# Copying the two halves of each tile's attention values through SP's DMA queue in place of POOL

## The chip, the cores and the metric

The kernel runs on one core of one Trainium2 chip. The metric is the device time of one execution in microseconds, as the median of several runs. The core has five engines with an instruction queue each: TensorE (PE, matmuls; PEld is its weight load), VectorE (DVE), ScalarE (ACT), GpSimd (POOL) and SyncE (SP, which here only issues DMAs). They meet through semaphores.

## The reference

Two blocks follow each other on x of 2 x 1024 x 128 float32, each with a layer norm ahead of and behind it and a residual sum: a gated linear attention, and two layers of local attention with a gated feed-forward part. The change lies in the local attention, 8 heads of 64, in windows of 64 tokens:

```python
def local_attention(q, k, v):
    b, h, n, d = q.shape
    w = n // WINDOW
    bq = q.reshape(b, h, w, WINDOW, d) * QK_SCALE
    bk = k.reshape(b, h, w, WINDOW, d)
    bv = v.reshape(b, h, w, WINDOW, d)
    def look_around(t):
        p = jnp.pad(t, ((0, 0), (0, 0), (1, 0), (0, 0), (0, 0)))
        return jnp.concatenate([p[:, :, :w], p[:, :, 1:]], axis=3)
    bk, bv = (look_around(bk), look_around(bv))
    ...
    sim = jnp.einsum('bhwid,bhwjd->bhwij', bq, bk)
    sim = jnp.where(mask, -jnp.finfo(sim.dtype).max, sim)
    attn = jax.nn.softmax(sim, axis=-1)
    out = jnp.einsum('bhwij,bhwjd->bhwid', attn, bv)
    return out.reshape(b, h, n, d)

def _layer(x, wqkv, qs, ksc, wo, lg, lb, w1, b1, w2, b2):
    h = shift_token(x)
    qkv = h @ wqkv
    ...
    o = local_attention(q, k, v)
    x = x + o @ wo
    h = shift_token(x)
    ...
    h = a * jax.nn.gelu(g, approximate=False)
    x = x + h @ w2 + b2
    return x

x = x + _layernorm(_L0_attn_ref(_layernorm(x), ...))
x = x + _layernorm(_L0_ffn_ref(_layernorm(x), ...))
```

Each window of queries looks at its own window of keys and values and at the one before it.

## The kernel before

Tokens are taken in tiles of 128 partitions, two windows of 64 each. The two batches alternate, so the 16 tiles of a layer are n = 0 to 15, and tile n - 2 holds the tokens ahead of tile n. The count over both layers is N = 16 l + n. The second window of a tile (partitions 64 to 127, w = 1 in `weigh_values`) looks at both halves of its own tile, which lie as they are in `v_cur`, one buffer for even and one for odd tiles, 8 heads of 64 columns and a column of ones (VC = 65), 520 columns. The first window (w = 0) looks at the first half of its own tile and the second half of tile n - 2; these are brought together in `v_mix`, four slots of 520 columns. The lower 64 partitions of a slot are filled from `v_cur` of tile n, the "own" half, and the upper 64 from `v_cur` of tile n - 2, the "past" half.

Every engine runs a fixed order, written by hand. For one tile, in steps k, the attention part is: TensorE projects q and k (two tiles ahead) and v (one ahead, `project_v`); ACT copies v from PSUM into `v_cur` (`copy_v_cur`, L1416); DVE rotates q and k (L1909), POOL adds the two rotated parts (`rotate_add`, L475) and scales them by the inverse norms of ACT (`scale_qk`, L483, after ACT's L1379); TensorE transposes them (L900), computes scores, DVE subtracts the row maxima, ACT takes exponentials, TensorE transposes the probabilities (L942), and `weigh_values` (L628 with `v_mix` and `v_cur`) multiplies them with the values. DVE divides by the row sums, TensorE transposes and projects the result (L967, L628 with `wo_sb`), and DVE adds it to the stream into `middle` (`add_attention`, L1971, which counts `mid_ready`). SP then copies `middle`, half of its columns shifted by one token, into `hcat` with three DMAs (L334 of 128 partitions, L336 of 127 and L338 of one), and from there the feed-forward part begins.

The copies into `v_mix` are two POOL instructions per tile: `mix_values` (L492) for the own half and `keep_values` (L503) for the past half, counted by `vlow_ready` and `vup_ready`. TensorE waits for them in `weigh_values`, and ACT in `copy_v_cur` before it overwrites a `v_cur` buffer. In a step POOL does `scale_qk`, the two copies, `normalise_z` (L511) and `rotate_add`, in that order.

The last two tiles of a layer (14 and 15) are not in the loop: in `drain` every engine interleaves them with the first hidden blocks of the feed-forward part. There TensorE's order is: `project_v(15)`, `scores(15)`, `weigh_values(14)`, `project_o(13)`, `transpose_probs(15)`, `transpose_o(14)`, `weigh_values(15)`, then `hidden_block(l, 0, 1)`, `transpose_o(15)`, `project_o(14)` and so on.

Of the kernel before, what the change touches and what calls it, by code (L numbers as in the profile page):

```python
# [24 lines left out]
def build_program(nc, x, Wq, Wk, Wv, Wg, Wgk1, Wgk2, bgk2, Wo, rms_w,  # L25
# [26 lines left out]
    with ctx:  # L52
# [53 lines left out]
        def tile_of(buf, n):  # L106
# [72 lines left out]

        d = sems("d_ident d_const d_masks d_x0 d_x1 d_x2 d_low d_qk d_vg d_out_w d_gcols d_rms d_qkv d_cols d_scales d_tab d_ffn d_even d_odd d_out")  # L180
        s = sems(
# [9 lines left out]
            "table_ready cos_ready xtr_done ht_ready qk_done rot_ready sq_ready ss_ready ssc_ready ssl_ready inv_ready "  # L191
            "add_ready qr_ready qkt_done qkt_ready v_done vcur_ready vlow_ready vup_ready sc_done max_ready sub_ready "
            "p_ready pt0_done pt1_done pt0_ready pt1_ready pv_done rec_ready on_ready ot_done ot_ready wo_done mid_ready "
# [80 lines left out]
        def _(sp):  # L274
# [39 lines left out]
            with nc.allow_non_contiguous_dma(reason="per-partition columns of the small vectors"):  # L314
# [3 lines left out]
                for l in range(DEPTH):  # L318
                    for half in range(2):
# [6 lines left out]
                                       ).then_inc(d["d_cols"], 16)  # L326

            for l in range(DEPTH):
                for n in range(NT):
                    N = NT * l + n  # L330
                    at = (n % 4) * D
                    sp.wait_ge(s["mid_ready"], N + 1)
                    wait(sp, s["zn_ready"], N - 3)
                    sp.dma_start(hcat[:, at:at + D // 2], middle[:, (n + 2) * D:(n + 2) * D + D // 2]  # L334
                                 ).then_inc(d[("d_even", "d_odd")[n % 2]], 16)
                    sp.dma_start(hcat[1:P, at + D // 2:at + D], middle[0:P - 1, (n + 2) * D + D // 2:(n + 3) * D]  # L336
                                 ).then_inc(d[("d_even", "d_odd")[n % 2]], 16)
                    sp.dma_start(hcat[0:1, at + D // 2:at + D], middle[P - 1:P, n * D + D // 2:(n + 1) * D]  # L338
                                 ).then_inc(d[("d_even", "d_odd")[n % 2]], 16)

            ov = res[:, :].rearrange("p (n d) -> p n d", d=D)
# [13 lines left out]
        def _(pool):  # L355
# [108 lines left out]
            for l in range(DEPTH):  # L464
# [20 lines left out]

                def mix_values(n, par):

                    N = base + n
                    W_ = AH * VC
                    wait(pool, s["vcur_ready"], N + 1)  # L490
                    wait(pool, s["pv_done"], N - 3)
                    pool.tensor_scalar(v_mix[0:W, (n % 4) * W_:(n % 4 + 1) * W_], v_cur[0:W, par * W_:(par + 1) * W_],  # L492
                                       1.0, 0.0, ALU.mult, ALU.add).then_inc(s["vlow_ready"], 1)

                def keep_values(n, par):

                    N = base + n
                    W_ = AH * VC
                    wait(pool, s["vcur_ready"], N + 1)
                    wait(pool, s["pv_done"], N - 1)  # L500
                    wait(pool, s["vlow_ready"], N + 1)
                    at = (n + 2) % 4 * W_
                    pool.tensor_scalar(v_mix[W:P, at:at + W_], v_cur[W:P, par * W_:(par + 1) * W_], 1.0, 0.0, ALU.mult, ALU.add  # L503
                                       ).then_inc(s["vup_ready"], 1)
                    wait(pool, s["vup_ready"], N + 1)

                def normalise_z(n, par):
# [6 lines left out]
                def step(k, par):  # L514
                    staged(scale_qk, k, par, 1)
                    staged(mix_values, k, par, 0)
                    staged(keep_values, k, par, 0)
                    staged(normalise_z, k, par, -3)
                    staged(rotate_add, k, par, 2)
                def attention_beside_last_pairs():  # L520
# [30 lines left out]
                    scale_qk(1, 1)  # L551
                    mix_values(0, 0)
                    keep_values(0, 0)
                    normalise_f(4, 0)
# [4 lines left out]
                    add_y(7, 1)  # L559
                    mix_values(1, 1)  # L560
                    keep_values(1, 1)
                    rotate_add(3, 1)
                    scale_qk(3, 1)
                    normalise_f(7, 1)
                    mix_values(2, 0)
                    keep_values(2, 0)
                    rotate_add(4, 0)
# [18 lines left out]
                pool.wait_ge(s["half_ready"], 1)  # L586
                pool.wait_ge(s["vup_ready"], base + NT)
                for n in (NT - 3, NT - 2, NT - 1):
                    rstd_of_z(n)
                    normalise_z(n, n % 2)  # L590
                if l + 1 < DEPTH:
                    pool.wait_ge(s["rot_ready"], base + NT)
                    pool.wait_ge(s["vup_ready"], base + NT)
                    for i in range(4):
                        cos_part(l + 1, i)
                        sin_part(l + 1, i)

            pool.wait_ge(s["vup_ready"], DEPTH * NT)

# [26 lines left out]
        def _(pe):  # L626
# [222 lines left out]
            for l in range(DEPTH):  # L849
# [95 lines left out]
                def weigh_values(n, par):  # L945
                    N = base + n
                    wait(pe, s["qkt_ready"], capped(N + 2, base + NT))
                    wait(pe, s["vcur_ready"], N + 1)
                    wait(pe, s["vlow_ready"], N + 1)
                    wait(pe, s["vup_ready"], base + max(n - 1, 0))  # L950
                    for a in range(2):
# [215 lines left out]
        def _(act):  # L1167
# [183 lines left out]
            for l in range(DEPTH):  # L1351
# [57 lines left out]
                def copy_v_cur(n, par):  # L1409
                    N = base + n  # L1410
                    wait(act, s["v_done"], N + 1)
                    wait(act, s["pv_done"], N - 1)
                    wait(act, s["vlow_ready"], N - 1)
                    wait(act, s["vup_ready"], N - 1)
                    o = v_cur[:, par * AH * VC:(par + 1) * AH * VC].rearrange("p (h e) -> p h e", e=VC)
# [811 lines left out]
```

## Time and profile before

| | us |
|---|---|
| median of 3 runs | 440.18 |
| lowest and highest | 439.87, 440.25 |
| the profiled execution | 440.01 |
| its span on the core | 437.9 |
| TensorE busy in the span | 409.5 |
| DVE busy | 339.5 |
| ACT busy | 305.5 |
| POOL busy | 292.6 |

Times within the trace are counted from the start of the span. A row of a timeline gives the start, the time taken, the engine, the line and the tensors written and read; what stands in brackets at its end is the idle time of the engine just ahead and what released it. Matmuls overlap each other, and the end of one is modelled, so a busy TensorE is not TensorE at its peak. The chain is the work that ended last, followed back from the end of the kernel to whatever released each piece.

### The profile page before, as it was taken

To read this page: it belongs to the slowest core of one execution; us is meant where nothing else is said; L and a number is where in the kernel's file an instruction comes from. 1 tells how busy PE (TensorE), PEld (TensorE's weight loads), DVE (VectorE), ACT (ScalarE), POOL (GpSimd) and SP (SyncE) were. 2 spreads that over 40 slices of the span, in tenths; PEclk is the share of its full clock that TensorE was granted. 3 is DMA by queue.
4 is the path that set the end of the run, shared out by engine and by line. 5 is a ranking of instruction groups with operands and counts; after the bars stand their busy time and mean duration, and the time that the engine had idled before them with its cause. 6 is when DMAs were issued, how large, how long until landed. Compare 5 with 4: busy or idle time off the path is not lost.

```text
span 437.9 us, 13201 instructions
## 1 busy us (share of the span) xinstructions
PE 409.5 (94%) x4851; PEld 291.2 (66%) x4851; DVE 339.5 (78%) x720; ACT 305.5 (70%) x677; POOL 292.6 (67%) x287
## 2 busy tenths in 40 slices
PE   3898999879999999999999999999999999999993
PEld 2566666656776777777766666677777777776563
DVE  3678867879898888988845377898889889855676
ACT  2677768758878887887773347678878878865322
POOL 3578957899978778776723536677777767761425
PEclk9999999999999999999999999999999999999998
DMA  7930000000000000000000000000000000000012
GB/s 190 327 70 3 2 3 3 3 1 2 8 15 8 7 13 9 8 12 10 7 7 14 0 2 2 7 8 8 12 10 7 11 12 8 8 8 13 8 35 61
DMA packets 21038, 10.37 MB, mean 24 GB/s; under 512 B 13236, under 2 KB 20208, under 8 KB 20976
## 3 DMA queue, kind: packets, MB, share of 16 engines
q1 hardware_dynamic: 20400, 9.14, 7.7%
q8 instruction: 40, 0.66, 0.6%
q10 hardware_dynamic: 576, 0.39, 0.3%
q14 instruction: 22, 0.18, 0.1%
HBM read 6.38 MB, written 1.05 MB: 17 GB/s over the span
## 4 chain that ended last, share of the span: by engine, by line
PE 73%; issue 5%; DVE 4%; ACT 3%; POOL 2%; DVEq 0%; POOLq 0%; ACTq 0%
PE psum L628 55%; PE psum L900 6%; PE psum L942 6%; PE psum L967 3%; PE psum L987 1%; PE psum L873 1%; ACT probs_t L1400 1%; DVE neg_max L1937 1%; POOL zn L511 1%; ACT qk_t L1387 1%; ACT sq L1368 0%; POOL rstd_z L578 0%; POOL ping L446 0%; PE psum L754 0%; DVE probs L1944 0%
## 5 line engine op out<-in xcount | busy, mean ns | idle before, releaser
L475 POOL TENSOR_TENSOR qr<-rot 128x1024 f32<-128x1024 f32 x32 | 75.8, 2367 | 29.4 <-DVE rot L1909 24.7
L628 PE MATMUL psum<-wqkv_sb,h_t 128*128 128x512 f32 x192 | 93.0, 595 | 0.0
L483 POOL TENSOR_TENSOR qr<-qr,inv 128x1024 f32<-128x1024 f32 x32 | 60.8, 1901 | 33.3 <-ACT inv L1379 33.2
L1917 DVE TENSOR_REDUCE ss<-sq 128x16 f32<-128x1024 f32 x32 | 39.0, 1219 | 14.8 <-ACT sq L1368 14.7
L1393 ACT ACTIVATE probs<-probs 128x512 f32<-128x512 f32 x64 | 39.4, 631 | 15.0 <-DVE probs L1944 14.6
L1937 DVE TENSOR_REDUCE neg_max<-psum 128x4 f32<-128x512 f32 x64 | 41.5, 685 | 10.4 <-PE psum L628 10.3
L628 PEld LDWEIGHTS psum<-v_mix,probs_t 128*64 128x64 f32 x512 | 32.2, 138 | 21.4 <-issue 19.8
L628 PE MATMUL psum<-z_t,w_sb 128*128 128x512 f32 (+1 forms) x96 | 44.7, 595 | 0.0
L628 PEld LDWEIGHTS psum<-wqkv_sb,h_t 128*128 128x128 f32 x192 | 31.7, 191 | 16.3 <-issue 16.2
L1944 DVE TENSOR_TENSOR probs<-psum,neg_max 128x512 f32<-128x512 f32 x64 | 41.3, 681 | 0.2
L1909 DVE TENSOR_TENSOR rot<-psum,cos_t 128x1024 f32<-128x1024 f32 x32 | 39.0, 1217 | 2.7 <-PE psum L628 2.4
L900 PEld LDWEIGHTS psum<-consts,qr 128*128 128x128 f32 x256 | 29.5, 141 | 16.5 <-POOL qr L483 10.9
L1337 ACT ACTIVATE gelu<-psum,columns 128x512 f32<-128x512 f32 (+1 forms) x24 | 16.4, 685 | 33.6 <-PE psum L628 33.5
L1909 DVE TENSOR_TENSOR rot<-psum,sin_t 128x1024 f32<-128x1024 f32 x32 | 38.8, 1214 | 0.0
L1368 ACT ACTIVATE sq<-psum 128x1024 f32<-128x1024 f32 x32 | 33.4, 1042 | 5.1 <-DVE rot L1909 5.1
L1880 DVE SCALAR_TENSOR_TENSOR hid<-psum,columns,gelu 128x512 f32<-128x512 f32 (+1 forms) x24 | 18.0, 749 | 24.2 <-ACT gelu L1337 24.2
L628 PE MATMUL psum<-v_cur,probs_t 128*64 128x65 f32 x512 | 36.7, 225 | 0.0
L628 PE MATMUL psum<-v_mix,probs_t 128*64 128x65 f32 x512 | 36.6, 225 | 0.1
L1407 ACT ACTIVATE o_t<-psum 128x512 f32<-128x512 f32 x32 | 19.1, 597 | 24.7 <-PE psum L967 23.3
L1387 ACT ACTIVATE qk_t<-psum 128x1024 f32<-128x1024 f32 x32 | 32.7, 1023 | 3.6 <-PE psum L900 2.0
L1400 ACT ACTIVATE probs_t<-psum 128x512 f32<-128x512 f32 x64 | 34.8, 598 | 0.5 <-PE psum L942 0.5
L942 PE MATMUL psum<-consts,probs 128*128 128x128 f32 x256 | 33.8, 274 | 1.4 <-ACT probs L1393 1.3
(150 smaller groups left out, 966.8 us busy)
## 6 DMA issues: line engine op xcount, KB each, us to landing
wqkv_sb<-in_L_ffn_wqkv SPq DMA_DIRECT2D x1, 1536.0 KB, 9.3
hcat<-middle SPq DMA_DIRECT2D x32, 32.0 KB
out_x<-pong SPq DMA_DIRECT2D x8, 128.0 KB, 1.8
hcat<-middle SPq DMA_DIRECT2D x32, 31.8 KB
x_in<-in_L_attn_x SPq DMA_DIRECT2D x2, 384.0 KB, 4.7
w_sb<-in_L_ffn_w SPq DMA_DIRECT2D x1, 682.0 KB
cos_base<-rotary_cos SPq DMA_DIRECT2D x1, 512.0 KB, 5.0
sin_base<-rotary_sin SPq DMA_DIRECT2D x1, 512.0 KB, 5.9
```

Of the source, the lines that this page charges most:

```text
L475: pool.tensor_tensor(o, a, b[:, :, ::-1, :], ALU.add).then_inc(s["add_ready"], 1)
L483: pool.tensor_tensor(a, a, inv[:, :].unsqueeze(2).to_broadcast([P, 2 * AH, DH]), ALU.mult).then_inc(s["qr_ready"], 1)
L628: return pe.matmul(o, w, m, start=start, stop=stop, skip_group_check=skip)
L900: ins = pe.transpose(p_turn[:, c * P:(c + 1) * P], qr[:, at:at + P], ident)
L942: ins = pe.transpose(p_sc[:, a * 512 + c * P:a * 512 + (c + 1) * P], probs[:, at:at + P], ident)
L1387: act.activation(qk_t[:, at:at + 2 * INNER], p_turn[:, :], ACT.Copy).then_inc(s["qkt_ready"], 1)
L1393: act.activation(p, p, ACT.Exp).then_inc(s["p_ready"], 1)
L1400: act.activation(probs_t[:, a * 512:(a + 1) * 512], p_sc[:, a * 512:(a + 1) * 512], ACT.Copy).then_inc(s[("pt0_ready", "pt1_ready")[a]], 1)
L1909: ins = dve.tensor_tensor(o[:, :].rearrange("p (i h e) -> p i h e", i=2, e=DH), x, tab.unsqueeze(2).to_broadcast([P, 2, AH, DH]), ALU.mult)
L1917: dve.tensor_reduce(ss[:, 0:4 * AH:2], sq[:, :].rearrange("p (h e) -> p h e", e=DH), AX.X, ALU.add).then_inc(s["ss_ready"], 1)
L1937: dve.tensor_reduce(neg_max[:, a * PAIRS:(a + 1) * PAIRS], heads_of(p_sc, a), AX.X, ALU.max, negate=True).then_inc(s["max_ready"], 1)
L1944: dve.tensor_tensor(heads_of(probs, a, par * AH * P), heads_of(p_sc, a), neg_max[:, a * PAIRS:(a + 1) * PAIRS].unsqueeze(2).to_broadcast([ ...
```

## The change

The two POOL instructions per tile are gone, with their semaphores and the waits on them. In their place SP issues two DMAs per tile (`spread_values`, with the same source and destination), each with a semaphore of its own for even and for odd tiles. Before each pair SP waits for `vcur_ready` of the tile and for `pv_done` of tile n - 2. Within a layer, SP's order is now the copies of tiles 0 and 1, then for each tile n its three `hcat` DMAs followed by the copies of tile n + 2. TensorE in `weigh_values` and ACT in `copy_v_cur` wait for the new semaphores in place of the old ones, at the same places.

```diff
+            def spread_values(l, n):
+                N = NT * l + n
+                W_ = AH * VC
+                own, past = n % 4 * W_, (n + 2) % 4 * W_
+                sp.wait_ge(s["vcur_ready"], N + 1)
+                wait(sp, s["pv_done"], N - 1)
+                sp.dma_start(v_mix[0:W, own:own + W_], v_cur[0:W, n % 2 * W_:(n % 2 + 1) * W_]
+                             ).then_inc(d[("d_own_even", "d_own_odd")[n % 2]], 16)
+                sp.dma_start(v_mix[W:P, past:past + W_], v_cur[W:P, n % 2 * W_:(n % 2 + 1) * W_]
+                             ).then_inc(d[("d_past_even", "d_past_odd")[n % 2]], 16)
+
             for l in range(DEPTH):
+                spread_values(l, 0)
+                spread_values(l, 1)
                 for n in range(NT):
...
                     sp.dma_start(hcat[0:1, at + D // 2:at + D], middle[P - 1:P, n * D + D // 2:(n + 1) * D]
                                  ).then_inc(d[("d_even", "d_odd")[n % 2]], 16)
+                    if n + 2 < NT:
+                        spread_values(l, n + 2)
...
-                def mix_values(n, par):
-                    N = base + n
-                    W_ = AH * VC
-                    wait(pool, s["vcur_ready"], N + 1)
-                    wait(pool, s["pv_done"], N - 3)
-                    pool.tensor_scalar(v_mix[0:W, (n % 4) * W_:(n % 4 + 1) * W_], v_cur[0:W, par * W_:(par + 1) * W_],
-                                       1.0, 0.0, ALU.mult, ALU.add).then_inc(s["vlow_ready"], 1)
-                def keep_values(n, par):
...
                 def step(k, par):
                     staged(scale_qk, k, par, 1)
-                    staged(mix_values, k, par, 0)
-                    staged(keep_values, k, par, 0)
                     staged(normalise_z, k, par, -3)
                     staged(rotate_add, k, par, 2)
...
                     wait(pe, s["vcur_ready"], N + 1)
-                    wait(pe, s["vlow_ready"], N + 1)
-                    wait(pe, s["vup_ready"], base + max(n - 1, 0))
+                    wait(pe, d[("d_own_even", "d_own_odd")[n % 2]], 16 * (N // 2 + 1))
+                    wait(pe, d[("d_past_even", "d_past_odd")[n % 2]], 16 * (N // 2))
...
                     wait(act, s["pv_done"], N - 1)
-                    wait(act, s["vlow_ready"], N - 1)
-                    wait(act, s["vup_ready"], N - 1)
+                    wait(act, d[("d_own_even", "d_own_odd")[n % 2]], 16 * (N // 2))
+                    wait(act, d[("d_past_even", "d_past_odd")[n % 2]], 16 * (N // 2))
```

SP's queue at the end of layer 0, before: the `hcat` DMAs of tiles 13 and 14, three each.

```order
79 L334 DMA hcat<-middle 128x64 [waits zn_ready,mid_ready]
80 L336 DMA hcat<-middle 127x64
81 L338 DMA hcat<-middle 1x16x4
82 L334 DMA hcat<-middle 128x64 [waits zn_ready,mid_ready]
83 L336 DMA hcat<-middle 127x64
84 L338 DMA hcat<-middle 1x16x4
```

The same place of SP's queue in the changed kernel: `hcat` of tile 13, the copies of tile 15, `hcat` of tile 14.

```order
106 L348 DMA hcat<-middle 128x64 [waits zn_ready,mid_ready]
107 L350 DMA hcat<-middle 127x64
108 L352 DMA hcat<-middle 1x16x4
109 L335 DMA v_mix<-v_cur 64x520 [waits pv_done,vcur_ready]
110 L337 DMA v_mix<-v_cur 64x520
111 L348 DMA hcat<-middle 128x64 [waits zn_ready,mid_ready]
112 L350 DMA hcat<-middle 127x64
113 L352 DMA hcat<-middle 1x16x4
```

The two copies of tile 15 now stand behind the wait for `mid_ready` of tile 13 and its three DMAs.

TensorE's queue in the same drain, before: the transposed probabilities of tile 15, the transposed output of tile 14, then the first matmuls of `weigh_values(15)`.

```order
719 L942 MATMUL psum<-consts,probs 128x128 [waits p_ready]
720 L942 MATMUL psum<-consts,probs 128x128 x3
721 L967 MATMUL psum<-consts,o_n 128x128 [waits ot_ready,vcur_ready,on_ready]
722 L967 MATMUL psum<-consts,o_n 128x128 x3
723 L628 MATMUL psum<-v_mix,probs_t 64x65 [waits vup_ready,vlow_ready,pt0_ready,vcur_ready,qkt_ready]
724 L628 MATMUL psum<-v_cur,probs_t 64x65
725 L628 MATMUL psum<-v_mix,probs_t 64x65
```

The same place of TensorE's queue in the changed kernel.

```order
719 L926 MATMUL psum<-consts,probs 128x128 [waits p_ready]
720 L926 MATMUL psum<-consts,probs 128x128 x3
721 L951 MATMUL psum<-consts,o_n 128x128 [waits ot_ready,vcur_ready,on_ready]
722 L951 MATMUL psum<-consts,o_n 128x128 x3
723 L612 MATMUL psum<-v_mix,probs_t 64x65 [waits d_past_odd,d_own_odd,pt0_ready,vcur_ready,qkt_ready]
724 L612 MATMUL psum<-v_cur,probs_t 64x65
725 L612 MATMUL psum<-v_mix,probs_t 64x65
```

Nothing moves on TensorE; the first `v_mix` matmul waits for `d_past_odd` and `d_own_odd` in place of `vup_ready` and `vlow_ready`.

POOL's queue in one step in the middle of layer 0, before (L373 makes a part of the rotary tables).

```order
110 L483 TENSOR_TENSOR qr<-qr,inv 128x1024 [waits inv_ready,add_ready]
111 L492 TENSOR_SCALAR v_mix<-v_cur 64x520 [waits vcur_ready]
112 L503 TENSOR_SCALAR v_mix<-v_cur 64x520 [waits vlow_ready,pv_done,vcur_ready]
113 L511 TENSOR_SCALAR zn<-hcat,mv_z,rstd_z 128x128 [waits z_rstd,vup_ready]
114 L475 TENSOR_TENSOR qr<-rot1,rot2 128x1024 [waits qkt_done,rot_ready]
115 L373 TENSOR_TENSOR cos_t<-cos_base,scales 128x256
116 L483 TENSOR_TENSOR qr<-qr,inv 128x1024 [waits inv_ready,add_ready]
```

The same step on POOL in the changed kernel.

```order
104 L499 TENSOR_TENSOR qr<-qr,inv 128x1024 [waits inv_ready,add_ready]
105 L506 TENSOR_SCALAR zn<-hcat,mv_z,rstd_z 128x128 [waits z_rstd]
106 L491 TENSOR_TENSOR qr<-rot1,rot2 128x1024 [waits qkt_done,rot_ready]
107 L389 TENSOR_TENSOR cos_t<-cos_base,scales 128x256
108 L499 TENSOR_TENSOR qr<-qr,inv 128x1024 [waits inv_ready,add_ready]
```

The two copies are gone from between the scaling and `zn`, and `zn` no longer waits for the second of them.

## Rows read from the trace of the kernel before

**Rows 1.** The page: busy times, and the shares of the chain by engine.

```profile
PE 409.5 (94%) x4851; PEld 291.2 (66%) x4851; DVE 339.5 (78%) x720; ACT 305.5 (70%) x677; POOL 292.6 (67%) x287
...
PE 73%; issue 5%; DVE 4%; ACT 3%; POOL 2%; DVEq 0%; POOLq 0%; ACTq 0%
```

**Rows 2.** The chain in order of time (start, us, what): q and k projections.

```profile
148.39 1.72 PE psum L628 x4
...
156.86 1.72 PE psum L628 x4
```

**Rows 3.** By tile, `v_mix` on POOL: count, ns min/median/max, first and last start.

```profile
L492 POOL TENSOR_SCALAR v_mix<-v_cur x32: 614/618/622, 98.6 to 391.5; 64x520 f32<-64x520 f32 x32
...
L503 POOL TENSOR_SCALAR v_mix<-v_cur x32: 622/624/629, 99.4 to 392.3; 64x520 f32<-64x520 f32 x32
```

**Rows 4.** Who waited for whom: us in total, times, longest us.

```profile
POOL qr L483 <- ACT inv L1379: 33.2, 29, 4.0
...
PE psum L900 <- POOL qr L483: 0.7, 1, 0.7
...
PEld psum L900 <- POOL qr L483: 10.9, 29, 0.6
```

**Rows 5.** Timeline of one middle tile of layer 0: start us, us, instruction.

```profile
136.65 0.63 ACT L1416 ACTIVATE v_cur<-psum 128x512 f32<-128x512 f32 x1
...
137.18 0.87 SPq L338 DMA_DIRECT2D hcat<-middle  x1
...
145.06 0.27 PE L628 MATMUL psum<-v_mix,probs_t 128*64 128x65 f32 x1
```

**Rows 6.** DMA issues: KB each, median us from issue to landing.

```profile
out_x<-pong SPq DMA_DIRECT2D x8, 128.0 KB, 1.8
...
wvg_sb<-in_L_attn_Wg ACTq DMA_DIRECT2D x1, 128.0 KB, 3.1
```

**Rows 7.** Timeline, start of layer 1: `v_cur` of tile 0, first use of `v_mix`.

```profile
268.14 0.60 ACT L1416 ACTIVATE v_cur<-psum 128x512 f32<-128x512 f32 x1 [0.49 <-PE psum L628]
...
272.53 0.24 PE L628 MATMUL psum<-v_mix,probs_t 128*64 128x65 f32 x1
```

**Rows 8.** Timeline, drain of layer 0: tiles 13 (DVE, SP) and 15 (PE).

```profile
225.57 0.28 DVE L1971 TENSOR_TENSOR middle<-psum,ping 128x128 f32<-128x128 f32 x1
...
227.11 0.87 SPq L338 DMA_DIRECT2D hcat<-middle  x1
...
226.56 0.27 PE L628 MATMUL psum<-v_mix,probs_t 128*64 128x65 f32 x1
```

**Rows 9.** Timeline, drain of layer 1: the same two.

```profile
397.44 0.88 SPq L338 DMA_DIRECT2D hcat<-middle  x1
...
396.89 0.27 PE L628 MATMUL psum<-v_mix,probs_t 128*64 128x65 f32 x1
```

**Rows 10.** DMA throughput in GB/s, 227 to 232 us in 40 equal slices.

```profile
GB/s 98 154 10 0 0 8 18 18 18 18 18 18 16 20 19 18 18 18 18 15 0 0 0 131 0 0 0 0 0 0 0 0 0 0 0 0 0 0 0 0
```

**Rows 11.** Stretches: length, busy PE, PEld, DVE, ACT, POOL, granted clock, DMA share, GB/s.

```profile
226.50:262.00 35.50, 35.50 (x193) 22.20 (x192) 18.30 (x36) 16.00 (x28) 13.11 (x16) 1.00 0.03 7
...
396.90:412.00 15.10, 15.10 (x100) 9.70 (x99) 8.56 (x25) 7.78 (x13) 3.62 (x6) 1.00 0.07 14
```

**Rows 12.** TensorE's last matmuls, and a later stretch (columns as in rows 11).

```profile
427.00 4.18 PE L628 MATMUL psum<-w_sb,hid 128*128 128x128 f32 x36
...
435.00:436.00 1.00, 0.00 (x0) 0.00 (x0) 0.23 (x1) 0.00 (x0) 0.09 (x1) 0.50 0.00 0
```

**Rows 13.** Timeline of TensorE in the first 24 us.

```profile
5.59 0.37 PE L638 MATMUL psum<-consts,wgk_sb 128*16 128x128 f32 x1 [5.59 <-DMA wgk_sb<-in_L_attn_Wgk]
...
8.78 1.22 PE L628 MATMUL psum<-middle,wgk_sb 128*128 128x256 f32 x2 [0.52 <-ACT middle L1199]
...
11.50 1.99 PE L628 MATMUL psum<-wvg_sb,middle 128*128 128x512 f32 x4
...
15.71 0.70 PE L628 MATMUL psum<-middle,wgk_sb 128*128 128x256 f32 x2
```

More of the change, by code:

```diff
@@ L177, in build_program @@
         xo, res = x_in, stream[DEPTH - 1]
-        d = sems("d_ident d_const d_masks d_x0 d_x1 d_x2 d_low d_qk d_vg d_out_w d_gcols d_rms d_qkv d_cols d_scales d_tab d_ffn d_even d_odd d_out")
+        d = sems("d_ident d_const d_masks d_x0 d_x1 d_x2 d_low d_qk d_vg d_out_w d_gcols d_rms d_qkv d_cols d_scales d_tab d_ffn d_even d_odd d_own_even d_own_odd d_past_even d_past_odd d_out")
         s = sems(
@@ L191, in build_program @@
             "table_ready cos_ready xtr_done ht_ready qk_done rot_ready sq_ready ss_ready ssc_ready ssl_ready inv_ready "
-            "add_ready qr_ready qkt_done qkt_ready v_done vcur_ready vlow_ready vup_ready sc_done max_ready sub_ready "
+            "add_ready qr_ready qkt_done qkt_ready v_done vcur_ready sc_done max_ready sub_ready "
             "p_ready pt0_done pt1_done pt0_ready pt1_ready pv_done rec_ready on_ready ot_done ot_ready wo_done mid_ready "
@@ L484, in scale_qk @@
                                        ).then_inc(s["qr_ready"], 1)
-                def mix_values(n, par):
-                    N = base + n
-                    W_ = AH * VC
-                    wait(pool, s["vcur_ready"], N + 1)
-                    wait(pool, s["pv_done"], N - 3)
-                    pool.tensor_scalar(v_mix[0:W, (n % 4) * W_:(n % 4 + 1) * W_], v_cur[0:W, par * W_:(par + 1) * W_],
-                                       1.0, 0.0, ALU.mult, ALU.add).then_inc(s["vlow_ready"], 1)
-                def keep_values(n, par):
[L497 to L505, printed above, removed]
                 def normalise_z(n, par):
@@ L551, in attention_beside_last_pairs @@
                     scale_qk(1, 1)
-                    mix_values(0, 0)
-                    keep_values(0, 0)
                     normalise_f(4, 0)
@@ L559, in attention_beside_last_pairs @@
                     add_y(7, 1)
-                    mix_values(1, 1)
-                    keep_values(1, 1)
                     rotate_add(3, 1)
@@ L564, in attention_beside_last_pairs @@
                     normalise_f(7, 1)
-                    mix_values(2, 0)
-                    keep_values(2, 0)
                     rotate_add(4, 0)
@@ L586, in _ @@
                 pool.wait_ge(s["half_ready"], 1)
-                pool.wait_ge(s["vup_ready"], base + NT)
                 for n in (NT - 3, NT - 2, NT - 1):
@@ L592, in _ @@
                     pool.wait_ge(s["rot_ready"], base + NT)
-                    pool.wait_ge(s["vup_ready"], base + NT)
                     for i in range(4):
@@ L596, in _ @@
                         sin_part(l + 1, i)
-            pool.wait_ge(s["vup_ready"], DEPTH * NT)
             def rstd_of_out(t):
```

## The prediction

> **What bounds the kernel now.** I read the busy times first, then the chain of work that ended last, then who waits for whom where the change cuts in. TensorE is busy 94% of the span and POOL 67%; the chain that ended last is 73% TensorE and 2% POOL [rows 1]. In the middle of a layer the chain stays on TensorE: the same 1.72 us piece (the q and k projection) starts at 148.39 and again at 156.86, so a tile takes 8.47 us [rows 2]. POOL is not the bound there. A gain or a loss can only come where POOL or a copy of values releases TensorE: at the start of a layer and in its drain (the hand-written order for the last tiles).
>
> **Part 1, what POOL no longer does.** 32 times 0.618 us and 32 times 0.624 us, 39.7 us in all [rows 3]. But POOL has room already: 29 times it stands before its scaling (L483) until ACT's inverse norms are there, 33.2 us in all [rows 4]. Work taken from in front of such a wait lengthens the wait and starts nothing earlier. What TensorE's matmuls wait for POOL's `qr` is 0.7 us, once; the weight loads wait 10.9 us for it, under running matmuls [rows 4]. So part 1 gives back between 0 and 0.7 us. I take 0.1, near the lower end, since the row with 29 waits for ACT tells what POOL's start hangs on.
>
> **Part 2, two more DMAs per tile on SP, in the middle of a layer.** Each moves 64 partitions of 520 float32, 133 KB. They stand behind the three `hcat` DMAs of an earlier tile, the last of which is issued at 137.18 and takes SP 0.87 us, to 138.05. The next tile's values are in `v_cur` at 136.65 + 0.63 = 137.28, and TensorE first reads their `v_mix` part at 145.06 [rows 5]. SP issues the own half at about 138.1. From issue to landing the nearest rows, of 128 KB each, are 1.8 us for a pair of output tiles and 3.1 us for a weight load in the busy first microseconds [rows 6]. I take 2.1 us (reason below): landed at 140.2, by the dearer row at 141.2; 3.9 us are left by the worse of the two. The next `hcat` comes a tile later and finds SP free. The first two tiles of a layer have their copies ahead of any `hcat` in SP's order; the tightest is tile 0 of layer 1, in `v_cur` at 268.14 + 0.60 = 268.74 and read at 272.53 [rows 7]: landed at 270.8, or 271.8. TensorE and ACT exchange two waits for two, so their queues get no longer. All this costs 0; if the cover of 3.9 us were gone, each tile would pay what is over.
>
> **Part 3, the two drains.** Here SP's order decides. The copies of tile 15 are issued behind the `hcat` DMAs of tile 13, and these wait for `mid_ready` of tile 13, DVE's L1971. In the middle TensorE reads a tile's values 7.0 us after SP is through with those three DMAs (138.05 to 145.06 [rows 5]); in the drain it is there before they are issued. Layer 0: L1971 for tile 13 ends at 225.57 + 0.28 = 225.85. SP then issues the three `hcat` DMAs, the last until 227.11 + 0.87 = 227.98, and the own half at 228.02. With 2.1 us it lands at 230.1. TensorE was at these matmuls at 226.56 [rows 8]: a wait of 3.5 us. Layer 1: SP's third `hcat` issue ends at 397.44 + 0.88 = 398.32, the own half lands at 398.36 + 2.1 = 400.46, and TensorE was there at 396.89 [rows 9]: 3.6 us. Bounds of each: 3.2 us with the 1.8 of the output pair, 4.5 us with the 3.1 of the weight load. The past half of tile 15 is read by nobody, and the next `hcat` (tile 14) follows the products of tile 14, which come behind the wait, so its time on SP is hidden.
>
> Why 2.1 us and not 1.8: after the first `hcat` part (98 and 154 GB/s in the two slices of 0.125 us from 227.0, 1.1 us behind its issue) the part of 127 partitions moves at 18 GB/s, from about 227.6 to 229.5 [rows 10]. So slow a stream is one DMA engine of 16, or little more, and it would still be busy when the own half begins. That engine's share of the own half is 133 KB / 16 = 8.3 KB, 0.46 us at 18 GB/s: 229.5 + 0.46 = 229.96, and 0.1 for the count, 230.1, which is 2.1 us after the issue. The Trainium skill ("DMA: Bandwidth & Descriptors", section "Why a DMA increments its semaphore by 16 and not by 1") says that a copy of 127 partitions runs on one engine alone; by that rule, the trace agrees. Its section "Anatomy of one DMA" puts a fixed 2.0 us on a DMA (measured on another issuing path) plus the bytes over its bandwidth; by it a landing would be 2.3 us and the whole 447.5 us, an estimate.
>
> Does the wait reach the end? The next hidden blocks and the output transposes and projections of tiles 14 and 15 stand on TensorE behind `weigh_values` of tile 15. From 226.5 to 262.0 TensorE is busy 35.50 of 35.50 us, and from 396.9 to 412.0 it is 15.10 of 15.10 [rows 11]. There is no gap that could swallow the wait, and DVE's next work is the reciprocals of tile 15, which need these products. Both waits count whole.
>
> **The sum.** 3.5 + 3.6 - 0.1 = 7.0 us. The profiled execution took 440.01 us (span 437.9), the median of the runs is 440.18; 440.1 + 7.0 = 447.1 us.
>
> **The rivals.**
>
> (a) *TensorE's clock falls in the wait.* At the end of the trace the last matmul ends at 427.00 + 4.18 = 431.18 and the granted clock is 0.50 in the stretch 435 to 436 [rows 12]: at 1.2 GHz no more than 3.8 us after the last matmul. The waits are about that long. What it costs is seen at the start, where two 256-column matmuls take 1.22 us at 8.78 and 0.70 at 15.71, while four of 512 columns take 1.99 us at 11.50 already, near the 1.72 us of such four in the middle [rows 2, 13]. TensorE's first matmul starts at 5.59, so the low level held for at most 5.9 us of work and cost half of that, 2.9 us. In one drain: 450.0 us; in both: 452.9. Against it: a wait of 3.5 us between two busy stretches is shorter than the one at the end. The Trainium skill ("TensorE: Matmul & The Clock Gate", section "Part 1: The HAM clock gate") says that recent activity is judged in windows that are not aligned with the kernel; by that rule the same wait could bring the clock down in one execution and not in the next.
>
> (b) *Not slower.* TensorE's busy time is modelled, so the 10.9 us in which weight loads wait for POOL's `qr` [rows 4] might be real gaps. If POOL's copies were what delays `qr`, their end would give these back: 447.1 - 10.9 = 436.2 us, faster than before. It decides from 7.0 us given back on. Against it stands the row with 33.2 us: POOL starts this scaling when ACT is done, not when POOL is free.
>
> (c) *A short wait.* The own half moves beside the one slow engine and lands at the 1.8 us row or sooner, and the engines behind TensorE win some tenths after it: 2.9 us per drain, 445.9 us, down to 444.5.
>
> (d) *Late in every tile.* A landing over 7 us from issue would stop TensorE in the some 13 middle tiles of each layer, 26 us for each microsecond over. The 3.9 us of room speak against it.
>
> **How the numbers follow.** Forecast, 447.1 us (446 to 449): 0.68. Clock falls, 449.5 to 453: 0.17. Short wait, 444.5 to 446: 0.08. Late in every tile, over 453: 0.03. Not slower: 0.04, of it 0.03 faster and 0.01 within 0.2%. That 0.2%, 0.9 us, is about what a measurement of this kernel can tell from no change. The range takes in the forecast, the short wait and most of one fallen clock, 444.5 to 451.0 us; the fall in both drains, the late copies and the case without a loss are left out. Slower by more than 0.2%: 0.68 + 0.17 + 0.08 + 0.03 = 0.96.
>
> **What would show it.** In the changed profile: TensorE idle once per layer before the `v_mix` matmuls of tile 15, 3.5 us, with SP's own-half issue right behind the third `hcat` issue of tile 13; no such wait at another tile; 8.47 us per tile as before; POOL's busy time down by 39.7 us and its waits for ACT and DVE up. The prediction would be wrong if that wait were under 2.5 us, if the granted clock left 1.00 before the last microseconds, if a middle tile became shorter or longer, or if the stretch behind the wait got part of it back.

## The result

The changed kernel takes 453.41 us (median of 6 runs, 452.11 to 457.39) where the kernel before takes 440.06 (6 runs, 439.68 to 440.35): 1.0274 times as long, interval 1.0232 to 1.0317. In a later series of runs it took 452.89 us (5 runs, 452.46 to 457.54), 1.0255 times [1.0201, 1.0308] the kernel before beside it. The forecast was 447.1 us with a range to 451.0, so the time lies above it. The sign and the place were right; the loss is 13.3 us and not 7. Of the runs told of here, three disturbed ones are left out: two of over 1,000 us (one of e1, one of e2) and one of e3 of 451.30 us.

The profiled execution took 455.39 us, its span is 453.2. These are lines of its page, to set beside [rows 1, 3]: the busy times, the granted clock of TensorE in 40 equal slices (9 is 90% of full speed or more), the chain, and the DMA issues of the copies (64 of them, 130 KB, median 2.4 us from issue to landing). The last line is the spread of that landing over all 64:

```profile
PE 417.3 (92%) x4851; PEld 295.4 (65%) x4851; DVE 339.4 (75%) x720; ACT 305.6 (67%) x677; POOL 253.7 (56%) x223
...
PEclk9999999889999999999989999999999999996998
...
PE 73%; issue 6%; DVE 4%; ACT 3%; POOL 2%; DVEq 0%; ACTq 0%; POOLq 0%
...
v_mix<-v_cur SPq DMA_DIRECT2D x64, 130.0 KB, 2.4
```
```profile
DMA to landing us min/median/max: 2.2/2.4/3.8
```

POOL has 38.9 us less to do (39.7 were forecast), and TensorE is busy 7.8 us longer with the same 4851 matmuls: it did not only wait, it also worked more slowly. The middle of a layer has not changed. The two pieces of [rows 2] are 8.48 us apart, where they were 8.47:

```profile
151.60 1.72 PE psum L612 x4
...
160.08 1.72 PE psum L612 x4
```

POOL's relief went into its own waits, as the view of who waited for whom says. The first line below is of the kernel before, the others are of the changed one. TensorE's weight loads wait for `qr` about as long as in [rows 4], 10.7 us and 10.9:

```profile
POOL qr L475 <- DVE rot L1909: 24.7, 24, 7.8
```
```profile
POOL qr L491 <- DVE rot L1893: 70.6, 30, 7.8
...
POOL qr L499 <- ACT inv L1363: 35.5, 30, 4.0
...
PEld psum L884 <- POOL qr L499: 10.7, 28, 0.6
```

The loss is made in the drains. Ahead of the matmuls that read `v_mix`, TensorE stood idle twice in the whole execution, for 7.8 us in all, and never in the kernel before:

```profile
  issue: 7.8, 2
```

The next views are SP's timeline in layer 0's drain, then the chain there, then the chain in layer 1's:

```profile
230.31 0.84 SPq L352 DMA_DIRECT2D hcat<-middle  x1
231.26 0.53 SPq L335 DMA_DIRECT2D v_mix<-v_cur  x1
```
```profile
229.84 3.90 issue
233.73 4.69 PE psum L612 x36
238.42 0.44 PE psum L951 x4
```
```profile
405.75 3.89 issue
409.64 5.71 PE psum L612 x36
```

The own half of tile 15 is issued right behind the third `hcat` copy of tile 13, and TensorE waits 3.9 us in each drain (the line "issue" is time in which the engine waited for nothing that the profile shows by name; the matmul behind it is the first that reads `v_mix` of tile 15). Behind the wait stands a piece of 36 matmuls (the weighing of tile 15 and a hidden block) that takes 4.69 and 5.71 us. Where the clock stays up behind a wait, it takes 3.07 (experiments 3 and 4). The stretches say why (columns as in [rows 11]):

```profile
229.80:233.80 4.00, 0.10 (x3) 0.10 (x4) 0.00 (x0) 2.69 (x4) 0.00 (x0) 1.00 0.38 83
234.30:237.60 3.30, 3.30 (x24) 1.99 (x20) 1.56 (x3) 0.00 (x0) 0.00 (x0) 0.50 0.00 0
405.80:409.60 3.80, 0.00 (x0) 0.00 (x0) 0.00 (x0) 2.60 (x4) 0.00 (x0) 0.84 0.40 86
409.80:415.00 5.20, 5.20 (x36) 3.04 (x36) 1.56 (x3) 0.00 (x0) 0.00 (x0) 0.50 0.01 3
```

In layer 0 the granted clock is still at 2.4 GHz (1.00) all through the wait and is at 1.2 GHz (0.50) behind it, when TensorE has work again. In layer 1 it falls within the wait.

**The sum of the profiled execution.** Its span is 15.3 us longer. The first `v_mix` matmul of tile 15 moved from 226.56 [rows 8] to 233.73, which is 7.17 us: 3.22 us were lost before the drain and 3.95 in the wait (the chain says 3.90; in the kernel before this matmul starts under the end of the transposition ahead of it). In layer 1 it moved from 396.89 [rows 9] to 409.64, 12.75 us: 8.80 of it was there before the wait, and 3.95 is the wait again. So 8.80 - 7.17 = 1.63 us were lost behind the first wait, and 15.3 - 12.75 = 2.6 behind the second. These are the excesses over 3.07 us of the two pieces above. The 3.22 us ahead of the drain belong to two stretches in which the clock was at 1.2 GHz with TensorE at work:

```profile
88.00:90.00 2.00, 2.00 (x3) 0.66 (x2) 1.04 (x4) 1.78 (x9) 2.00 (x3) 0.50 0.00 0
...
98.00:100.00 2.00, 2.00 (x22) 1.67 (x15) 1.21 (x3) 0.00 (x0) 2.00 (x2) 0.50 0.53 113
```

The first lies ahead of the first copy (issued at 97.8 us), so no copy causes it. Such falls come in some executions and not in others. The variant e1 below, which has no wait in its drains, had three of them in its profiled execution, two ahead of its first copy (99.3 us); it took 444.78 us where its shortest took 439.63:

```profile
72.00:76.00 4.00, 4.00 (x7) 2.02 (x8) 1.69 (x3) 2.36 (x8) 3.79 (x5) 0.57 0.00 0
88.00:92.00 4.00, 3.80 (x36) 2.04 (x37) 2.52 (x7) 2.81 (x11) 4.00 (x4) 0.65 0.00 0
100.00:104.00 4.00, 4.00 (x16) 2.80 (x13) 3.13 (x8) 1.52 (x3) 4.00 (x5) 0.64 0.31 67
```

The kernel before most likely has them too: of its 39 later runs 16 took over 441 us, up to 445.25, with a mean granted clock of 0.986 to 0.994 where the others have 0.994 to 0.998. Without such falls the changed kernel has 440.06 + 3.95 + 3.95 + 1.63 + 2.6 = 452.2 us, and the shortest of its 11 runs took 452.11.

### The profile page after: what moved, and what is told of

It reads as the page before. It is cut to its first block, busy times and chain, and to the rows that moved or that the text cites. A ratio compares the mean times of both kernels' runs of the same rounds, so it can differ in the third digit from the quotient of the medians.

```text
span 453.2 us, 13164 instructions
## 1 busy us (share of the span) xinstructions
PE 417.3 (92%) x4851; PEld 295.4 (65%) x4851; DVE 339.4 (75%) x720; ACT 305.6 (67%) x677; POOL 253.7 (56%) x223
## 4 chain that ended last, share of the span: by engine, by line
PE 73%; issue 6%; DVE 4%; ACT 3%; POOL 2%; DVEq 0%; ACTq 0%; POOLq 0%
PE psum L612 54%; PE psum L884 6%; PE psum L926 5%; PE psum L951 3%; PE psum L971 1%; PE psum L857 1%; ACT probs_t L1384 1%; DVE neg_max L1921 1%; POOL zn L506 1%; ACT qk_t L1371 1%; ACT sq L1352 0%; POOL rstd_z L565 0%; POOL ping L462 0%; PE psum L738 0%; DVE probs L1928 0%
## 5 line engine op out<-in xcount | busy, mean ns | idle before, releaser
L612 PE MATMUL psum<-wqkv_sb,h_t 128*128 128x512 f32 x192 | 95.1, 606 | 0.0
L612 PEld LDWEIGHTS psum<-v_mix,probs_t 128*64 128x64 f32 x512 | 33.4, 141 | 29.3 <-issue 27.7
L1377 ACT ACTIVATE probs<-probs 128x512 f32<-128x512 f32 x64 | 39.4, 631 | 15.3 <-DVE probs L1928 14.9
L612 PE MATMUL psum<-z_t,w_sb 128*128 128x512 f32 (+1 forms) x96 | 47.7, 628 | 0.0
L612 PE MATMUL psum<-v_mix,probs_t 128*64 128x65 f32 x512 | 37.8, 229 | 7.8 <-issue 7.8
L884 PEld LDWEIGHTS psum<-consts,qr 128*128 128x128 f32 x256 | 29.6, 141 | 15.6 <-POOL qr L499 10.7
L612 PE MATMUL psum<-v_cur,probs_t 128*64 128x65 f32 x512 | 37.9, 229 | 0.0
```

What stands on the lines that cost most here:

```text
L612: return pe.matmul(o, w, m, start=start, stop=stop, skip_group_check=skip)
L884: ins = pe.transpose(p_turn[:, c * P:(c + 1) * P], qr[:, at:at + P], ident)
L1377: act.activation(p, p, ACT.Exp).then_inc(s["p_ready"], 1)
```

## Experiments

All are edits of the changed kernel unless it is said otherwise. They ran in three series, each on a chip of its own: e1, e3, e5 and the first runs of e2; then e4, e6, e7 and the changed kernel again; then e8 and e2 again. Beside each stands its ratio to the kernel before, run in the same series.

**1. The copies of tile 15 ahead of the `hcat` copies of tile 13.** All copies stay on SP; only the order of the last two changes.

```diff
                 for n in range(NT):
                     N = NT * l + n
                     at = (n % 4) * D
+                    if n == NT - 3:
+                        spread_values(l, NT - 1)
                     sp.wait_ge(s["mid_ready"], N + 1)
...
-                    if n + 2 < NT:
+                    if n + 3 < NT:
```

> The changed kernel, but SP issues the copies of tile 15 ahead of the hcat DMAs of tile 13 instead of behind them; all other copies stay where they were. Theory A (the loss is SP's order in the two drains, and TensorE's clock which falls in those waits): v_mix of tile 15 lands some 2.4 us after v_cur is ready, before TensorE comes to it; no wait, granted clock 1.00 in both drains, 440.1 us (439.5 to 441). Theory B (64 more DMAs of 133 KB slow the kernel wherever they stand, by traffic or by what they do to the clock at the start of layer 0, where the profiled run of the changed kernel lost 3.2 us): 443 us or more with the drains mended. Theory C (POOL's freed time was worth something that the drains hid): below 439.5 us.

Measured: 439.96 us (9 runs, 439.63 to 445.22), against 440.05 of the kernel before (19 runs, 439.60 to 445.25); ratio 0.9983 [0.9933, 1.0032]. The wait is gone: the chain of layer 0's drain goes from the transposition to the 36 matmuls without a pause.

```profile
230.96 0.44 PE psum L953 x4
231.39 3.00 PE psum L614 x36
```

All 64 copies are still there, and POOL still has some 39 us less to do. Together the two change nothing beyond the half per cent of the interval; the loss hangs on the place of tile 15's copies in SP's queue.

**2. One copy alone.** The kernel before, with POOL's copies, but the own half of tile 15 issued by SP behind tile 13's `hcat`.

```diff
+                    if n == NT - 3:
+                        W_ = AH * VC
+                        sp.wait_ge(s["vcur_ready"], NT * (l + 1))
+                        sp.wait_ge(s["pv_done"], NT * (l + 1) - 2)
+                        sp.dma_start(v_mix[0:W, (NT - 1) % 4 * W_:((NT - 1) % 4 + 1) * W_], v_cur[0:W, W_:2 * W_]
+                                     ).then_inc(d["d_own"], 16)
...
                 def mix_values(n, par):
+                    if n == NT - 1:
+                        return
```

POOL no longer makes that half, and the waits of TensorE, ACT and POOL are adapted to it (not shown).

> The kernel before, with one copy per layer moved: only the own half of tile 15 goes over SP's queue, behind the hcat of tile 13; POOL does the other 62 copies as before. Theory A: the whole loss of the drains is there, waits of 3.7 to 4.0 us in both and a fallen clock in them (1.6 to 2.7 us each): 450.5 us (448 to 453). Theory B (the number of DMAs makes the loss): two DMAs more cost nothing that can be seen, 440 to 442 us.

Measured: 455.72 us (4 runs, 451.89 to 457.14), ratio 1.0268 [1.0193, 1.0343], the whole loss of the change. The chain in the two drains:

```profile
230.00 3.90 issue
233.90 5.72 PE psum L639 x36
...
407.10 3.93 issue
411.03 5.72 PE psum L639 x36
```

Two copies of 64, one per layer, make the change's loss. Of the expectation the place held and the price did not: 450.5 us counted the two waits and one fallen clock, and here it fell in both drains and, as the next rows show, at 73 to 75 and 90 to 92 us, where this program is still that of before:

```profile
73.00:75.00 2.00, 2.00 (x4) 0.81 (x3) 1.36 (x3) 1.89 (x5) 1.90 (x3) 0.50 0.00 0
90.00:92.00 2.00, 2.00 (x4) 0.93 (x3) 0.97 (x3) 1.75 (x10) 2.00 (x3) 0.50 0.00 0
```

**3. The wait filled with idle work.** Does the wait cost 3.95 us, and the clock the rest? TensorE repeats the four transpositions ahead of the wait nine times over, which writes the same values again.

```diff
-                def transpose_o(n, par):
+                def transpose_o(n, par, times=1):
...
-                    for c in range(PAIRS):
+                    for c in list(range(PAIRS)) * times:
...
-                    transpose_o(k, 0)
+                    transpose_o(k, 0, 9)
                     weigh_values(last, 1)
```

> The changed kernel, but TensorE does the transposes of tile 14's output in the drain nine times over (36 in place of 4, 3.5 us more) where it would wait for the copy of tile 15; the result is the same. The wait for the copy stays, its idle time is filled. Theory A1 (part of the loss is the clock that falls because TensorE idles): the granted clock stays at 1.00 in both drains, and the time is 440.1 + 2 x 3.95 = 448.0 us, 5 us below the changed kernel, or up to 451 with the falls at the start of layer 0. Theory A2 (the low clock in the drains has another cause, for instance the DMA traffic): the time stays at 452 to 454 us.

> The changed kernel with tile 14's 4 transpositions before the wait repeated to 36 in both drains (the values are written again, nothing else changes), once more, for an undisturbed profile. Theory A (without a fall of TensorE's clock the waits cost 3.95 + 3.89 us and no more): 447.7 to 448.0 us in most executions, granted clock at 2.4 GHz from the start of layer 0's drain to the end of the last matmuls, wait rows at tile 15 below 0.5 us behind the repeated transpositions. Theory B (the lateness costs more than the waits): above 449.5 us with the clock up.

Measured: 447.72, 447.83 and 450.90 us in the first series, ratio 1.0126 [1.0052, 1.0200]; in the later one 447.93 us (4 runs, 447.79 to 451.50), ratio 1.0169 [1.0115, 1.0223]. The profile is of the later one. In layer 0 the wait is full but for 0.39 us, and the 36 matmuls behind it take 3.07 us; in layer 1 the clock stays at 1.00:

```profile
225.96 3.93 PE psum L951 x36
229.89 0.39 issue
230.28 3.07 PE psum L612 x36
```
```profile
404.00:408.00 4.00, 3.57 (x43) 2.35 (x42) 1.65 (x3) 2.86 (x4) 0.00 (x0) 1.00 0.15 31
```

Tile 15 is as late as ever, 7.9 us over the two drains, and 440.06 + 7.9 = 447.96 is what is measured. Work that does nothing makes the kernel 5 us faster in the median and 4.4 at the lowest (452.11 and 447.72). This splits the loss: 7.9 us are lateness, the rest is the clock, and in the drains the clock falls because TensorE stands idle.

**4. Three sizes of the wait.** The copies of tile 15 behind tile 13's wait for `mid_ready` but ahead of its three `hcat` copies (e3), then behind the first of the three (e8), and e3 with four times the transpositions, `transpose_o(k, 0, 4)` (e7). The edit of e3, then that of e8; both have `n + 3 < NT` at the end of the loop, as e1.

```diff
                     wait(sp, s["zn_ready"], N - 3)
+                    if n == NT - 3:
+                        spread_values(l, NT - 1)
                     sp.dma_start(hcat[:, at:at + D // 2], middle[:, (n + 2) * D:(n + 2) * D + D // 2]
```
```diff
                                  ).then_inc(d[("d_even", "d_odd")[n % 2]], 16)
+                    if n == NT - 3:
+                        spread_values(l, NT - 1)
                     sp.dma_start(hcat[1:P, at + D // 2:at + D], middle[0:P - 1, (n + 2) * D + D // 2:(n + 3) * D]
```

> The changed kernel, but the copies of tile 15 are issued right after the wait for tile 13's add and ahead of its three hcat DMAs. Theory A: the copy starts 2.3 us earlier and lands some 2.0 us after its issue, as that of tile 0 does; the wait shrinks from 3.95 to about 1.5 us per drain, the clock holds, 440.1 + 3.0 = 443.1 us (442.3 to 444). If a wait of 1.5 us is enough to bring the clock down: 446 us or more. If the copy lands late whatever stands ahead of it (2.5 us and more): a wait of 2 us, 444.1 us.

> The short-wait kernel (tile 15's copies ahead of tile 13's three hcat copies; TensorE waits 1.65 us in each drain; 443.18 us where the clock stayed up, 446 to 451 us in 8 of 10 runs) with the 4 transpositions before the wait repeated to 16, which fill 1.3 us of it. Theory A (its runs above 443.3 us come from falls of TensorE's clock in or behind the waits of 1.65 us): most runs at 443.2 to 443.6 us, median below 444.5. Theory B (they come from falls elsewhere, at 70 to 103 us, as in runs of the kernel before in that call that took up to 445.25 us): median 446 us or more, as unfilled. The transpositions repeated are not part of the computation; they write the same values again.

> The two copies of tile 15 stand behind the first of tile 13's three hcat copies instead of behind all three: issued 0.65 + 0.84 us and two gaps, so 1.65 us, earlier. Theory S (the copy itself takes 2.3 to 2.4 us to land, whatever stands ahead of it): wait of 3.9 - 1.65 = 2.25 us in each drain, so 444.5 us where the clock stays up. Theory H (the 127-partition copy ahead of it takes 0.4 us of the landing): wait of 1.85 us, 443.7 us. Clock: if the chance of a fall grows with the wait, more runs fall than with 1.65 us (8 of 10) and each fall costs 1.6 to 2.7 us: median 447.5 to 450 us.

| wait per drain, us | filled | runs | lowest, us | median, us | ratio |
|---|---|---|---|---|---|
| none (e1) | | 9 | 439.63 | 439.96 | 0.9983 |
| 1.65 (e3) | no | 9 | 443.18 | 446.58 | 1.0111 [1.0064, 1.0158] |
| 1.65 (e7) | yes | 10 | 443.16 | 443.43 | 1.0063 [1.0037, 1.0088] |
| 2.31 (e8) | no | 4 | 447.66 | 450.51 | 1.0203 [1.0137, 1.0268] |
| 3.9 (after) | no | 11 | 452.11 | 453.34 | 1.0274, 1.0255 |
| 3.9 (e2) | yes | 7 | 447.72 | 447.83 | 1.0126, 1.0169 |

The chain at tile 15 in layer 0 of e3, and of e8:

```profile
226.29 1.65 issue
227.95 3.07 PE psum L614 x36
```
```profile
229.85 2.32 issue
232.17 3.07 PE psum L614 x36
```

In e3's profiled execution the clock never left 2.4 GHz before the end, and it took 443.18 us: 440.06 + 2 * 1.65 = 443.4. Of its nine runs seven took 446.14 us or more, 3.0 us and more above the lowest, with a mean clock of at most 0.987. With the wait filled (e7) the longest of ten stands 2.1 us above the lowest. This speaks for a fall in or behind some of the waits of 1.65 us, but does not show it: no profile caught one, e3 and e7 ran in different series, their intervals overlap, and the falls at the start of layer 0 lengthen a run by as much. In e3's series the kernel before and e1, which have no wait, were 3.0 us or more above their lowest in 9 of 28 runs; in e7's series the kernel before was so in 3 of 13.

At 2.31 us a profile did catch one. In e8's profile layer 0's wait left the clock up, and behind layer 1's, of the same length, it was down:

```profile
232.20:236.00 3.80, 3.80 (x45) 2.73 (x46) 1.56 (x4) 1.02 (x2) 0.00 (x0) 1.00 0.05 9
402.60:404.90 2.30, 0.01 (x2) 0.04 (x2) 0.00 (x0) 2.27 (x4) 0.00 (x0) 1.00 0.60 128
405.00:408.30 3.30, 3.30 (x34) 2.54 (x35) 1.34 (x3) 0.26 (x1) 0.00 (x0) 0.50 0.05 10
```

In or behind the waits of 3.8 to 4.0 us it fell in every drain profiled, 8 of 8 (twice the changed kernel, e4 and e5). It can come early: in layer 0 of e4 (experiment 5), whose wait begins at 226.69, the mean clock of the first 2.0 us is 0.85, so it had been down for some 0.6 us of them (an estimate from that mean):

```profile
226.70:228.70 2.00, 0.00 (x0) 0.00 (x0) 0.00 (x0) 1.97 (x4) 0.00 (x0) 0.85 0.11 25
```

**5. Nothing behind the own half.** What makes the time from issue to TensorE 0.4 us longer than forecast? The past halves of tiles 14 and 15, read by nobody, are left out.

```diff
-                sp.dma_start(v_mix[W:P, past:past + W_], v_cur[W:P, n % 2 * W_:(n % 2 + 1) * W_]
-                             ).then_inc(d[("d_past_even", "d_past_odd")[n % 2]], 16)
+                if n < NT - 2:
+                    sp.dma_start(v_mix[W:P, past:past + W_], v_cur[W:P, n % 2 * W_:(n % 2 + 1) * W_]
+                                 ).then_inc(d[("d_past_even", "d_past_odd")[n % 2]], 16)
```

TensorE and ACT wait for accordingly smaller counts (not shown).

> The half copies of tiles 14 and 15 that no later tile reads (the past halves) are left out, so that nothing is queued on SP behind the own half of tile 15. It lands 2.37 us after its issue in the profile of after, against 1.93 us for the first copy of the layer. Theory P (the past half behind it takes a share of the engines): it lands 1.9 to 2.0 us after its issue, the wait at TensorE is 3.5 us in place of 3.9, and the time falls by 0.8 to about 452.6 us. Theory H (the copies of hcat ahead of it do, or the size): 2.3 to 2.4 us, wait 3.9 us, time within 0.3 us of the changed kernel's in the same call.

Measured: 452.52 us (4 runs, 452.10 to 452.78), against 452.89 of the changed kernel in the same series; ratio 1.0252 [1.0206, 1.0297]. The chain in layer 0:

```profile
226.69 3.97 issue
230.65 5.07 PE psum L613 x36
```

From SP's issue of the own half to TensorE's start it is 2.51 us here and 2.62 in layer 1, no less than in the changed kernel, so the copy behind plays no part. (The expectation's 1.93 us for the first copy of the layer is not borne out either: of the 64 landings none is under 2.2.) What stands ahead hardly matters. SP issues the own half in e3 with no `hcat` copy before it, in e8 behind one:

```profile
225.55 0.46 SPq L335 DMA_DIRECT2D v_mix<-v_cur  x1
```
```profile
229.68 0.55 SPq L335 DMA_DIRECT2D v_mix<-v_cur  x1
```

From the issue to TensorE's start it is 2.40 us in e3, 2.49 in e8 and 2.47 in the changed kernel. The three `hcat` copies ahead cost it less than 0.1 us.

**6. Useful work in the wait.** In both drains TensorE does a hidden block and the projection of tile 14 ahead of the weighing of tile 15.

```diff
-                    weigh_values(last, 1)
                     pe.wait_ge(s["pt0_ready"], base + NT)
                     pe.wait_ge(s["pt1_ready"], base + NT)
                     hidden_block(l, 0, 1)
-                    transpose_o(last, 1)
                     project_o(k, 0)
+                    weigh_values(last, 1)
+                    transpose_o(last, 1)
```

> The changed kernel with TensorE's order changed in both drains: the hidden block (0,1) of 1.83 us and the output projection of tile 14 of 0.9 us run before the weighing of tile 15, in its wait. The transposition of tile 15 then follows its weighing at once, and waits for VectorE's 0.21 + 0.69 us and the semaphores, some 1.2 us. Theory A (the waits and the falls behind them make the loss): the waits of 3.9 us become about 1.2 us, 1.5 us is won in each drain, and the clock stays up in most executions: 440.06 + 2 * 2.4 = 444.9 us, up to 449 where it falls in one of the drains by chance. Theory B (the fall follows any disturbance here): 449 us and more. Theory C (the late tile 15 delays the end of the layer by itself): no gain against the changed kernel, 452 us.

Measured: 445.63 us (4 runs, 444.54 to 447.81), ratio 1.0103 [1.0047, 1.0158]. The chain in layer 0:

```profile
229.93 2.85 PE psum L612 x12
232.78 0.70 issue
233.48 1.17 PE psum L612 x32
...
234.91 0.70 DVE o_n L1948
```

Of the 3.9 us 0.7 are left. DVE's division of tile 15 is now bare instead of hidden, and the clock stays up in both drains of the profiled execution. By the lowest runs the late copy costs 2.2 us per drain here, 6.0 in the changed kernel. No variant beats the kernel before; the best of them, e1, equals it.

## Why the prediction failed

**What bounds the kernel, parts 1 and 2: held.** A tile takes 8.48 us (8.47 before), no middle tile has such a wait, and POOL's 38.9 us went into its own waits. Rival (b) fell with the row of `qr`, 10.7 us after and 10.9 before; rival (c) fell with waits of 3.9 us; rival (d) never came near. The relief of 0.1 us is too small to be seen: e1, with the relief and all the DMAs, equals the kernel before within half a per cent.

**Part 3, order and place: held.** SP issued the own half 0.95 us after the third `hcat` issue began, as forecast (228.02, and 231.26 less the 3.22 of shift is 228.04).

**Part 3, the landing: too small.** The step "so slow a stream ... would still be busy when the own half begins" gave 2.1 us from issue to TensorE. It is 2.47, and 2.40 in e3 without any such stream ahead, so the slow stream does not set it. The two waits are 7.9 us and not 7.1, which is 0.8 of the 6.3 us missing. The nearest row, 1.8 us of a pair of output tiles, was for a copy to DRAM; the copies from SBUF to SBUF take 2.2 us at the least. Why they take longer was not tried. The estimate of 2.3 us from the Trainium skill's figure ("DMA: Bandwidth & Descriptors", "Anatomy of one DMA") was nearer than the forecast; the landing row above has a median of 2.4.

**Part 3, "Both waits count whole": held.** Experiment 3 has 447.9 us with the wait and without the clock, 7.9 over before. The sum of the prediction was a sum for a kernel whose clock doesn't fall, and for that one it was 0.8 us short.

**The step that failed: rival (a) was the case, and in both drains.** The sum put the clock at nothing. Rival (a) was given 0.17, with 452.9 us for both drains. Against it the prediction put "a wait of 3.5 us between two busy stretches is shorter than the one at the end". That was an argument from a row that gives only an upper bound: the clock was seen low 3.8 us after the last matmul, and nothing in the trace of before said how much earlier it could fall. In e4's it fell within the first 2.0 us of a wait, and in e8's it was down behind a wait of 2.31 us. The prediction had named the sign itself: the granted clock left 1.00 before the last microseconds. The Trainium skill ("TensorE: Matmul & The Clock Gate", "Part 1: The HAM clock gate") says that activity is judged in windows that are not aligned with the kernel. By that rule the same wait can bring the clock down once and not the next time; e8's profile agrees, where one of two waits of 2.3 us did and the other did not. At 3.9 us none of the eight drains profiled was spared. The price was mis-sized the other way: 2.9 us per fall were forecast, 1.63 and 2.6 came. The terms are then 7.9 + 4.2 = 12.1, and the 1 us more in the median most likely comes from the falls at the start of layer 0. That the rival's 452.9 us lies so near the measured 453.41 is in part luck: its waits were 0.8 us too short, its falls 1.6 us too dear, and the falls at the start of layer 0 it did not have.

**The range.** It left out the fall in both drains as the more remote case. But the two waits have the same length, so what can bring the clock down in one can do so in the other; at 3.9 us it did in both drains of all four profiles. The two cases should not have been taken as one common and one rare, and the range should have reached 453.

## What to carry to other kernels

When a copy moves to another queue, look at the last tiles of a loop, where the order is its own: what stands ahead of it there may be work that the consumer overtakes. Price a bare wait of TensorE with two terms, the wait and the clock behind it, and if the wait can't be removed, put other matmuls into it, useful ones first, idle ones if need be. Where a stretch comes twice, do not take the cost in both as the remote case: what causes it once is there the second time.

## What the runs showed of the hardware

- In a kernel whose TensorE is otherwise busy 94% of the span, all eight profiled waits of 3.8 to 4.0 us and one of two of 2.31 us had the granted clock fall from 2.4 to 1.2 GHz in or behind them. Two waits of 1.65 us took it down in neither drain of the one execution profiled; the longer runs (median 446.58 us, 443.43 with the waits filled) speak for falls in others, and this stays open.
- Repeated transpositions in the wait kept the clock up: 447.83 us in the median of 7 runs, 453.34 in that of the 11 with the bare waits of 3.9 us.
- The fall need not lie in the wait: in layer 0 of the changed kernel the clock was 1.00 to the end of the wait and 0.50 from 234.3 to 237.6 us, with TensorE busy throughout. One fall behind a wait cost 1.6 to 2.7 us (the piece of 36 matmuls took 4.66 to 5.73 us in place of 3.07).
- The clock also falls in the first 104 us in some executions, in e5 where the program is that of before. It is the likely reason why 16 of 39 runs of the kernel before took over 441 us, up to 445.25; no profile of that kernel caught one. What sets it off was not tried and stays open.
- A copy of 64 partitions of 520 float32 from SBUF to SBUF reached its reader in the drains 2.4 to 2.6 us after SP's issue, whether 0, 1 or 3 copies were issued just ahead of it. From issue to landing the 64 copies of an execution took 2.2 us at the least, 2.4 in the median and 3.8 at the most.
